# A decoder layer's mixture of experts computed by picked experts only

## The reference

```python
scores = jax.nn.sigmoid(xt.astype(jnp.float32) @ gate_w.T)      # 16 experts
biased = scores + gate_b
_, idx = lax.top_k(biased, TOPK)                                 # 4 of 16
w = jnp.take_along_axis(scores, idx, axis=-1)
w = w / jnp.sum(w, axis=-1, keepdims=True) * ROUTE_SCALE         # 2.5
...                                                              # comb: w scattered, 0 where not picked
def expert_body(y, args):
    w13_e, w2_e, c_e = args
    h = _silu_and_mul(xt @ w13_e.T)                              # 256 -> 2 x 128
    return (y + c_e[:, None] * (h @ w2_e.T), None)               # 128 -> 256
...
y = y + _silu_and_mul(xt @ w13_s.T) @ w2_s.T                     # shared expert, all tokens
```

## Time and profile before

| | us |
|---|---|
| median of three runs | 772.29 |
| the profiled execution | 776.83 |
| span of its instructions | 774.0 |
| cross-attention, first to last score step | 351.1 to 442.8 |
| experts, first projection to last down matmul | 454.9 to 765.4 |
| after the last matmul | 8.6 |

### The profile page before, as it was taken

One profiled execution on the slowest core, in us unless ns is written; L12 is line 12 of the kernel. 1 busy time (PEld: TensorE's weight loads), 2 busy tenths in 40 slices (PEclk: granted clock), 3 DMA queues, 4 the chain that ended last, 5 costly groups with the idle time before them and its releaser, 6 DMA issues.

```text
span 774.0 us, 12337 instructions
## 1 busy us (share of the span) xinstructions
PE 724.4 (94%) x4376; PEld 481.3 (62%) x4376; DVE 557.6 (72%) x1195; ACT 378.7 (49%) x639; POOL 306.4 (40%) x364
## 2 busy tenths in 40 slices
PE   6778899999999999889999998989999999999994
PEld 3434433443443423545777787878888888888883
DVE  0278878878878830876887834898788777877777
ACT  2222476676676677234444434644444444444541
POOL 8314222424424426240122204754545455445542
PEclk9979999999999999999999978999999999999999
DMA  4766954534533000620000000000000000000000
GB/s 152 155 165 141 219 146 61 88 56 60 86 58 58 4 18 17 267 95 1 1 1 1 1 1 1 1 0 1 1 1 22 8 1 1 28 0 2 8 21 28
DMA packets 22572, 38.24 MB, mean 49 GB/s; under 512 B 7248, under 2 KB 10576, under 8 KB 22128
## 3 DMA queue, kind: packets, MB, share of 16 engines
q1 hardware_dynamic: 22512, 37.47, 20.9%
...
...
## 4 chain that ended last, share of the span: by engine, by line
PE 71%; DVE 16%; issue 4%; ACT 3%; DMA 3%; SPq 1%; POOL 1%; POOLq 0%; DVEq 0%; ACTq 0%
PE ps L1135 19%; PE ps L1233 10%; PE ps L1030 8%; PE ps L1006 8%; PE ps L989 6%; DVE neg_max L713 5%; PE ps L1172 3%; PE ps L1153 3%; DVE x_tok L889 3%; PE ps L1044 2%; PE ps L1187 2%; PE ps L1162 2%; PE ps L994 2%; DMA stacks<-qk_parts 1%; PE ps L1205 1%
## 5 line engine op out<-in xcount | busy, mean ns | idle before, releaser
L713 DVE TENSOR_REDUCE neg_max<-ps 128x1 f32<-128x512 f32 (+3 forms) x304 | 181.8, 654 | 44.8 <-PE ps L994 28.3
L1135 PE MATMUL ps<-x_split,w_split 128*128 128x512 f32 x816 | 204.5, 400 | 0.7 <-POOL w_split L521 0.5
L595 ACT ACTIVATE temps<-ps 128x1024 f32<-128x1024 f32 (+1 forms) x192 | 147.5, 812 | 77.2 <-PE ps L1006 77.2
L1135 PEld LDWEIGHTS ps<-x_split,w_split 128*128 128x128 f32 x816 | 152.0, 192 | 32.1 <-issue 1.4
L521 POOL TENSOR_TENSOR w_split<-stacks,w_split 128x512 fp32r<-128x512 f32 x70 | 90.4, 1291 | 129.5 <-ACT w_split L629 129.5
L989 PE MATMUL ps<-stacks 96*128 96x512 bf16 (+3 forms) x384 | 105.4, 331 | 13.8 <-DMA stacks<-qk_parts 7.4
L1233 PE MATMUL ps<-w_split,h_split 128*128 128x256 f32 x816 | 110.5, 285 | 6.5 <-DVE x_tok L889 5.2
L1233 PEld LDWEIGHTS ps<-w_split,h_split 128*128 128x128 f32 x816 | 106.3, 190 | 15.2 <-issue 10.6
L482 POOL TENSOR_SCALAR_AFFINE_SELECT temps<-temps 128x256 f32<-128x256 f32 x128 | 52.2, 411 | 147.2 <-ACT temps L595 146.2
L889 DVE SCALAR_TENSOR_TENSOR x_tok<-ps,o_norm,x_tok 128x256 f32<-128x256 f32 x256 | 105.6, 474 | 0.1
L635 ACT ACTIVATE temps<-ps 128x512 f32<-128x512 f32 x68 | 40.6, 597 | 112.7 <-PE ps L1135 112.5
...
## 6 DMA issues: line engine op xcount, KB each, us to landing
stacks<-qk_parts SPq DMA_DIRECT2D x96, 128.0 KB, 5.7
...
stacks<-in_w SPq DMA_DIRECT2D x1, 2176.0 KB, 18.4
...
temps<-row_sums SPq DMA_DIRECT2D x32, 64.0 KB, 2.4
out_tokens<-x_tok SPq DMA_DIRECT2D x16, 128.0 KB, 1.7
```

Of the source, the lines that this page charges most:

```text
L595: nc.scalar.activation(pt[:, n % 4, :, 0:w], ps[:, 2 + 2 * (n % 2):4 + 2 * (n % 2), 0:w], ACT.Exp, scale=SCALE).then_inc(b_exp, 1)
L713: nc.vector.tensor_reduce(nmx[:, c, h0:h0 + nh, i], ps[:, A_BANKS[n % 3], 0:w * nh].rearrange("p (h k) -> p h k", h=nh), axis=AX.X, op=ALU ...
L1135: last = nc.tensor.matmul(ps[:, 2 * part + e % 2, :], w13s[:, split_buf(e), wp, k, P * part:P * part + P], xs[:, bass.ds(c, 1), xp, k, :], ...
```

## The change

The 16 routed experts are no longer run on all tokens. Each token's row, 273 words (256 of x, its 16 weights, its number), is written four times to a DRAM buffer `expert_slots`, to the next free slot of each picked expert's region: 64 indirect DMAs from POOL ("C" in the list, 16 for each four tiles), each with one destination index per partition and 1092 B a row. The slot numbers are ranks, counted by small matmuls (`ranks`, "K") and picked out by DVE (`slot_rows`, "I"). All four routings ("R", "Q", "W") are now in the list of cross-attention.

Each expert's last block is filled up by 16 DMAs of 128 padding rows, whose addresses SP reads into a register (`value_load`). DVE computes a table of blocks (16 small operations); it goes through DRAM and comes back as a row. There are always 79 blocks of 128 slots: 64 full ones and 15 for the remainders. For each block SP reads its row address into a register and loads 128 x 1092 B; PE transposes it (T), multiplies it with the expert that a register names (U: 6 matmuls of 256 columns), transposes h (H), and multiplies down (D: 3 matmuls of 256 columns); ACT and DVE make the high and low parts; the weighted result is added by an indirect accumulating DMA from POOL to rows of a DRAM tensor. There are two such tensors, for even and odd blocks, cleared by DMAs. A block's accumulation is issued once that of two blocks before has landed. At the end both tensors are loaded (8 DMAs of 512 KB) and added to x by DVE, and all 16 tiles are normed and stored.

The weights are split once for each expert and kept: on ACT and POOL at tiles 8 to 15 of the first norm (`w_low` after `power`) and at the first eight "X" of cross-attention. The shared expert runs on all tokens in four chunks, at the end of cross-attention and after. Cross-attention's buffers are moved to make room.

```diff
+XR = D + E + 1
+REGION = T + P
+ROWS = E * REGION + P
+NBK = T * TOPK // P + E - 1
...
+LAGS = {"S": 0, "T": 2, "V": 4, "N": 4, "P": 5, "O": 5, "Y": 6, "Z": 7, "X": 8, "L": 9, "R": 9, "Q": 10, "W": 11,
+        "K": 12, "I": 12, "C": 12}
...
+    for s in range(-4, NBK):
+        for kind, b in (("U", s + 2), ("T", s + 4), ("H", s + 1), ("D", s)):
+            if 0 <= b < NBK:
+                out.append((kind, b))
...
+            for u in range(2):
+                sp.dma_start(acc[u].rearrange("(j p) d -> p j d", p=P),
+                             a["clear"].unsqueeze(1).to_broadcast([P, NT + 1, D])).then_inc(cleared, 16)
+            sp.dma_start(slots[E * REGION:ROWS, :], a["pad"]).then_inc(padded, 16)
...
+            sp.wait_ge(r_table, 1)
+            sp.dma_start(tables, tabI).then_inc(tab_out, 16)
+            sp.dma_start(marks, onehot[0:NBK + 1]).then_inc(tab_out, 16)
+            for q in range(4):
+                sp.wait_ge(scattered[q], 16 * TOPK * 4)
+            for e in range(E):
+                row = sp.value_load(prow[0:1, e:e + 1], min_val=0, max_val=ROWS - 2 * P)
+                sp.dma_start(slots[bass.ds(row, P), :], a["pad"]).then_inc(padded, 16)
+            sp.wait_ge(tab_out, 32)
+            sp.dma_start(tabrow, tables.rearrange("p u -> (p u)").unsqueeze(0)).then_inc(tab_in, 16)
+            sp.dma_start(ohb[:], marks.rearrange("b e -> (b e)").unsqueeze(0).to_broadcast([P, (NBK + 1) * E]))\
+              .then_inc(rows_in, 16)
+            sp.wait_ge(tab_in, 16)
+            sp.wait_ge(padded, 16 * (E + 1))
+            sp.wait_ge(xo_ready, 2 * NT)
+            for b in range(NBK):
+                if b >= XB:
+                    sp.wait_ge(xb_T, b - XB + 1)
+                    sp.wait_ge(c_ready, (b - XB) // XB4 + 1)
+                row = sp.value_load(tabrow[0:1, 2 * b + 1:2 * b + 2], min_val=0, max_val=ROWS - P)
+                sp.dma_start(xblk[:, b % XB, :], slots[bass.ds(row, P), :]).then_inc(xb_in[b % XB], 16)
+
+            sp.wait_ge(yb_ready, NBK)
+            sp.wait_ge(summed[0], 16 * ((NBK + 1) // 2))
+            sp.wait_ge(summed[1], 16 * (NBK // 2))
+            for c in range(4):
+                for u in range(2):
+                    sp.dma_start(accb[:, u, 4 * c:4 * c + 4, :],
+                                 acc[u][CH * c:CH * c + CH].rearrange("(j p) d -> p j d", p=P)).then_inc(ld_acc[c], 16)
...
+            def w_low(e):
+
+                pool.wait_ge(w_hi, 2 * e + 2)
+                for raw, high, low in zip(raw_of(e), part_of(e, 0), part_of(e, 1)):
+                    nc.gpsimd.tensor_tensor(low, raw, high, ALU.subtract).then_inc(w_lo, 1)
...
                 power(t)
-            pool.wait_ge(y_ready, NT)
+                if t >= W_TILE:
+                    w_low(t - W_TILE)
+            w_low(NT - W_TILE)
...
+                if kind == "X" and n < E - (NT - W_TILE):
+                    w_low(NT - W_TILE + 1 + n)
+                if kind == "L":
+                    x_low(n)
+                if kind == "C":
+                    pool.wait_ge(r_index, n + 1)
+                    pool.wait_ge(r_comb, n + 1)
+                    pool.wait_ge(ln_done, NT + 4 * n + 4)
+                    pool.wait_ge(filled, 13)
+                    for t in range(4 * n, 4 * n + 4):
+                        for k in range(TOPK):
+                            pool.indirect_dma_start(
+                                slots, bass.IndirectOffsetOnAxis(ridx[:, t, k:k + 1].bitcast(U32), 0),
+                                xe[:, t, :], None).then_inc(scattered[n], 16)
+
+            pool.wait_ge(cleared, 32)
+            for b in range(NBK):
+                pool.wait_ge(yb_kept[b % 2], b // 2 + 1)
+                pool.wait_ge(c_ready, b // XB4 + 1)
+                wait(pool, summed[b % 2], 16 * (b // 2))
+                pool.indirect_dma_start(acc[b % 2], bass.IndirectOffsetOnAxis(idxs[:, b:b + 1].bitcast(U32), 0),
+                                        yb[:, b % 4, :], None, compute_op=ALU.add).then_inc(summed[b % 2], 16)
...
+            for kind, b in BLOCKS:
+                if kind == "T":
...
+                    nc.scalar.activation(xsp[b % 3][:, 0].rearrange("p k s -> p (k s)"), ps[:, b % 2, 0:D],
+                                         ACT.Copy).then_inc(xb_hi, 1)
+                if kind == "U":
...
+                    nc.scalar.activation(gsil[:, b % 3, :], ps[:, 2 + b % 2, 0:INTER], ACT.Silu).then_inc(gu_silu, 1)
+                if kind == "H":
...
+                    nc.scalar.activation(hsp[:, b % 3, 0], ps[:, 4 + b % 2, 0:P], ACT.Copy).then_inc(hb_hi, 1)
+                if kind == "D" and b % 2 == 0:
+                    act.wait_ge(yb_ready, b + 1)
+                    act.wait_ge(c_ready, b // XB4 + 1)
+                    if b >= 4:
+                        act.wait_ge(summed[0], 16 * (b // 2 - 1))
+                    nc.scalar.activation(yb[:, b % 4, :], ps[:, 6, 0:D], ACT.Identity,
+                                         scale=cblk[:, b:b + 1]).then_inc(yb_kept[0], 1)
...
+            def slot_rows(q):
+
+                tiles = slice(4 * q, 4 * q + 4)
+                dve.wait_ge(r_rank, q + 1)
+                rank = ps[:, 5, D:D + 4 * E].rearrange("p (t e) -> p t e", t=4)
+                link(nc.vector.tensor_tensor(vrow, rank, mpick[:, tiles], ALU.mult))
...
+            def add_shared(c):
+
+                dve.wait_ge(moe_y, c + 1)
+                dve.wait_ge(scattered[c], 16 * TOPK * 4)
...
+            def block_weights(g):
...
+                link(nc.vector.tensor_tensor(ctmp[:, 0:n], xblk[:, at:at + n, D:D + E],
+                                             ohb[:, XB4 * g * E:(XB4 * g + n) * E].rearrange("p (u e) -> p u e", u=n),
+                                             ALU.mult))
+                link(nc.vector.reduce_sum(cblk[:, XB4 * g:XB4 * g + n], ctmp[:, 0:n], axis=AX.X))
+                nc.vector.tensor_copy(idxs[:, XB4 * g:XB4 * g + n].unsqueeze(2),
+                                      xblk[:, at:at + n, XR - 1:XR].bitcast(I32)).then_inc(c_ready, 1)
...
+            for kind, b in BLOCKS:
+                if kind == "T":
+                    dve.wait_ge(xb_hi, b + 1)
...
+                    nc.vector.tensor_tensor(xsp[b % 3][:, 1].rearrange("p k s -> p (k s)"), ps[:, b % 2, 0:D],
+                                            xsp[b % 3][:, 0].rearrange("p k s -> p (k s)"),
+                                            ALU.subtract).then_inc(xb_lo, 1)
+                    if b % XB4 == XB4 - 1 or b == NBK - 1:
+                        block_weights(b // XB4)
+                if kind == "U":
+                    dve.wait_ge(gu_silu, b + 1)
...
+                    nc.vector.tensor_tensor(hblk[:, b % 3, :], ps[:, 2 + b % 2, INTER:2 * INTER], gsil[:, b % 3, :],
+                                            ALU.mult).then_inc(hb_done, 1)
+                if kind == "H":
+                    dve.wait_ge(hb_hi, b + 1)
+                    nc.vector.tensor_tensor(hsp[:, b % 3, 1], ps[:, 4 + b % 2, 0:P], hsp[:, b % 3, 0],
+                                            ALU.subtract).then_inc(hb_lo, 1)
+                if kind == "D" and b % 2:
+                    dve.wait_ge(yb_ready, b + 1)
+                    if b >= 4:
+                        dve.wait_ge(summed[1], 16 * (b // 2 - 1))
+                    nc.vector.tensor_scalar(yb[:, b % 4, :], ps[:, 7, 0:D], cblk[:, b:b + 1], None,
+                                            ALU.mult).then_inc(yb_kept[1], 1)
+
+            def add_blocks(c):
+                tiles = slice(4 * c, 4 * c + 4)
+                dve.wait_ge(ld_acc[c], 32)
+                dve.wait_ge(y_added, 4 * c + 4)
+                nc.vector.tensor_tensor(x[:, tiles], x[:, tiles], accb[:, 0, tiles], ALU.add).then_inc(acc_in, 1)
+                dve.wait_ge(acc_in, 2 * c + 1)
+                nc.vector.tensor_tensor(x[:, tiles], x[:, tiles], accb[:, 1, tiles], ALU.add).then_inc(acc_in, 1)
...
+            add_blocks(0)
+            for c in range(4):
+                block_stats(c)
+                if c < 3:
+                    add_blocks(c + 1)
...
+            def ranks(q):
+
+                ranked[0] = q + 1
+                pe.wait_ge(r_chain, routed[q])
...
+            expert = {}
+            pe.wait_ge(tab_in, 16)
+            for kind, b in BLOCKS:
+                if kind == "T":
+                    pe.wait_ge(xb_in[b % XB], 16 * (b // XB + 1))
+                    if b >= 2:
+                        pe.wait_ge(xb_lo, b - 1)
                     else:
-                        down(c - 1, NE - 2 + e)
-
-            blocks(pe, experts)
-            down(T // CH - 1, NE - 2)
-            down(T // CH - 1, NE - 1)
+                        pe.wait_ge(g_silu, 3 + b)
+                    for k in range(KC):
+                        last = nc.tensor.transpose(ps[:, b % 2, P * k:P * k + P], xblk[:, b % XB, P * k:P * k + P],
+                                                   identf[:])
```

(33 more changed lines are left out.)

546 lines of the change are left out of this document (326 added, 220 removed).

## The result

The changed kernel is slower. Its median is 842.8 us (four runs, 838.3 to 845.47) against 775.5 for the kernel before beside it: a ratio of 1.086, 95% interval 1.077 to 1.096. In a second series it was 844.2 us, ratio 1.094 (1.089 to 1.099). The profiled execution took 841.62 us with a span of 839.9, 65.9 more than the 774.0 of before. The forecast was 788, with a range of 741 to 860; the likeliest case's own range, 775 to 815, does not hold the result.

The account below looks back on a forecast made before the run. PE was taken to bound the kernel, with 150 us to go if it still did; against that, five terms on a time line gave a span of 789.0 us against 774.0, so a predicted median of 788, range 741 to 860.

Parts of the forecast that it names:

- likeliest case: Whole kernel: slower, as POOL's scatters delay cross-attention and its accumulations pace the blocks; 775 to 815 us.
- low-clock rival: Blocks: PE at 1.2 GHz takes 3.0 us a block, 58 us more, 846; chance 0.17 together with long landing.
- one of the signs: Cross-attention trace: the last score step's start near 480 us instead of 443.
- C(1): Cross-attention: the second group of 16 scatters on POOL, forecast to start at 454.6 us.
- Term 1: First norm, tiles 8 to 15: POOL's weight splitting behind each power paces the tiles, 5 us.
- Term 2: Cross-attention: 16 scatters at 1.3 us hold up POOL's power; cycle 38.6 us instead of 23.5, last landed at 550.8.
- Term 3: Between scatters and blocks: 16 register reads and padding DMAs, 12 us, then landing and first block's load and way, 5.
- D(0): Blocks: the first block's down projection on PE, forecast at 573.4 us.
- Term 4: Blocks: POOL's accumulations, issue 1.3 and landing 3.2 us for two blocks, set 2.25 us a block, 175.5 us.
- Term 5: Tail: last accumulation 4.5 us, loading the sums, DVE's additions and norms; from 748.9 to 789.0 us.
- Quick landing: Blocks: accumulations land like a plain store in 1.8 us, 1.65 us a block, 47 us less, 741; chance 0.18.
- Short issue: Scatters and blocks: an indirect DMA costs POOL only 0.45 us, about 701 us; chance 0.09.

Follow-up runs that it names:

- run 5: Changed kernel with all 64 scatters issued after POOL's whole cross-attention list instead of 16 at each C: 854.6 us, ratio 1.106 to the kernel before.
- run 6: Changed kernel with each quarter's scatters issued two per step over the next eight steps, the last quarter's kept together: 804.2 us, ratio 1.039 to the kernel before.
- run 2: Changed kernel with the 16 padding DMAs issued before SP waits for the scatters instead of after: 828.1 us, ratio 1.069 to the kernel before.
- run 3: Changed kernel with three sums in DRAM instead of two, so an accumulation waits for b-3: 808.9 us, ratio 1.044 to the kernel before.
- run 4: Changed kernel with plain indirect writes in place of the blocks' accumulations, so its result is not the layer's: 807.6 us, ratio 1.043 to the kernel before.
- run 1: Changed kernel with the weight splitting of experts 0 to 8 moved from first norm to cross-attention steps 0 to 8: 829.85 us, ratio 1.073 to the kernel before.

## Why the prediction was right in sign and 55 us short

The sign, the place of the losses and the likeliest case's mechanism held: scatters queued ahead of `power`, padding exposed, blocks paced by issue and landing over two sums, a long tail. Runs 5 and 6 show the first, run 2 the second, runs 3 and 4 the third. The terms were too small, all five in the same direction. The wide range holds the result; 842.8 is near the low-clock rival's 846, but that is chance, as its mechanism (PE at 3.0 us a block) did not occur. Chance too is one of the signs: the last score step was to start near 480 us and did so at 480.2, but C(1) came 19 us later than forecast and the step 6.7 us behind it, not 25.

- **Term 1, first norm: 5 us forecast, 17 measured, 13 of them at the end (run 1).** I took POOL's own 2.7 us a tile as the price (8 x 0.7, which is 5.6). The step that failed is "the ACT side of the splitting, 1 us at 16 places, lies beside an engine 48% busy": its place in ACT's order, behind q copies that wait for PE, set when POOL could start (POOL waited 13.7 us for it). A busy share does not say what an instruction stands behind.
- **Term 2, scatter: 1.3 us an instruction came out (1.26), the cycle did not: 44.1 and 44.9 us instead of 38.6.** The 1.3 was luck: I had it from the row of a subtraction, and it is an issue of 0.96 and a gap of 0.30. The last cycle, which has little PE work in it, took 34.4, as forecast. The 5.5 to 6.3 us are PE's: I let DVE set the pace after the stall at 2.4 us a step, but after 7.7 us of waiting the granted clock is 0.65, and the first two steps are PE's, 11.2 us from the transpose to the end of Y where I had 4.8. The chain shows that PE is the link there; run 5, where no stall is, has the clock at 1.00 and 95.0 us for 31 steps. No run has the stall with the clock held up, so how the excess divides between the clock and PE's own 2.94 us a step is not shown.
- **Term 3: 12 us for the 16 DMAs became 20.** The register read was not the 0.3 us of my estimate but 0.27 and 0.15 with gaps, and the DMA with a register in its address takes 0.52 on SP where a plain one took 0.45; 1.27 against 0.75. Its bounds (0 to 0.45 for the register) did not hold the gaps. The way through T, U, H and D was 7.5 us, not 5 (601.5 to 609.0), at a clock of 0.50: I had counted block 0 alone, but in PE's order the U of blocks 1 and 2 stand ahead of D(0) too, 1.6 us each there.
- **Term 4: 2.25 us a block forecast, 2.38 measured.** The issue was 1.56, not 1.3; from its start to the landing it was 3.9 us and not 4.5, so the landing behind the issue was 2.3 and not 3.2; but 0.7 to 1.0 us pass from a landing to the next issue, which I had not counted. 3.9 + 0.85, the middle of the two, is 4.75 for two blocks, the 2.38 measured: that the forecast was close is luck, three errors that nearly cancel.
- **Term 5: 40 us forecast, 45.6 measured.** The load of the first quarter (5.4 us) and DVE's work were as costed, 28 us from the first loaded quarter to the end. But the last accumulation landed 12 us behind the last D and not 5, as it was still queued behind those before it.

**The rivals.** Quick landing was right in part: behind the issue the landing took 2.3 us, between the rival's 1.8 and my 3.2 and nearer to its own. It did not bring its time, as the longer issue and the uncounted 0.85 us took it back. The Trainium skill, page "DMA: Bandwidth & Descriptors", section "Anatomy of one DMA — SWDGE (gpsimd) path", gave an estimate of 2.3 us for this size. Taken as the landing behind the issue, as I did, the accumulation agrees; taken as the whole DMA, the plain scatter (2.6 from the issue's start) comes near and the accumulation (3.9) does not. The rival's price was off as well: run 4 saves 32 us of block time (185.3 to 153.7) and not 47, because PE's own block is 1.9 us and not 1.5; D's three matmuls take 0.55 us and not 0.36, and the transposes 0.52 and not 0.42. Short issue did not occur. The low clock did not decide in the blocks (0.94, and 1.00 as soon as the landings were out of the way), but it added to terms 2 and 3, where I had not looked for it. The Trainium skill, page "TensorE: Matmul & The Clock Gate", section "What's actually happening", has the throttled state as the default that activity releases; 0.50 in 575 to 609 us, behind the idle stretch, agrees.

What stays open: how much of the 0.94 in the blocks is a loss of its own. No run raised the clock and left the landings as they were.
